# Layer norm of the first stage: row work on 128x128 and squared sums, spread and high part arranged for it, in five rounds

## The reference, cut to what matters

```
def _ln(x, w, b):
    mu = jnp.mean(x, axis=-1, keepdims=True)
    var = jnp.var(x, axis=-1, keepdims=True)
    return (x - mu) * jax.lax.rsqrt(var + EPS) * w + b
...
zn = _ln(z, ln_in_w, ln_in_b)             # z = group norm of x
a = m * jax.nn.sigmoid(zn @ w_ag + b_ag) * (zn @ w_ap + b_ap)
b = m * jax.nn.sigmoid(zn @ w_bg + b_bg) * (zn @ w_bp + b_bp)
p = jnp.einsum('bikc,bjkc->bijc', a, b)
x = _ln(p, ln_out_w, ln_out_b) @ w_z + b_z
g = jax.nn.sigmoid(zn @ w_g + b_g)
return x * g
```

## Time and profile before

| | |
|---|---|
| median of 3 runs | 1107.92 us |
| profiled execution, its own time | 1107.85 us |
| its span (first to last instruction) | 1105.8 us |
| PE busy | 997.5 us (90%) |
| DVE busy | 804.0 us (73%) |
| ACT busy | 681.7 us (62%) |
| POOL busy | 556.9 us (50%) |
| granted TensorE clock, mean | 0.957 |

### The profile page before, as it was taken

One profiled execution on the slowest core, in us unless ns is written; L12 is line 12 of the kernel. 1 busy time (PEld: TensorE's weight loads), 2 busy tenths in 40 slices (PEclk: granted clock), 3 DMA queues, 4 the chain that ended last, 5 costly groups with the idle time before them and its releaser, 6 DMA issues.

```text
span 1105.8 us, 36355 instructions
## 1 busy us (share of the span) xinstructions
PE 997.5 (90%) x14204; PEld 780.1 (71%) x14204; DVE 804.0 (73%) x1270; ACT 681.7 (62%) x1102; POOL 556.9 (50%) x479
## 2 busy tenths in 40 slices
PE   5689798579999999996999997799999999789997
PEld 5543333248898888985999997587878787645554
DVE  6926988976786868767988888664646565567775
ACT  5747565365666656655676765484857667546665
POOL 0000644488092561904777774390937648146664
PEclk9989999869999999998999998799999999989999
DMA  9800000000301203069999760004031130599994
GB/s 349 317 9 1 0 1 0 1 2 4 134 24 78 78 22 134 4 181 231 226 208 203 180 149 1 2 4 154 5 104 54 46 111 4 167 196 285 294 276 153
DMA packets 173196, 121.32 MB, mean 110 GB/s; under 512 B 69764, under 2 KB 152068, under 8 KB 173064
## 3 DMA queue, kind: packets, MB, share of 16 engines
q1 hardware_dynamic: 173064, 119.34, 39.9%
HBM read 68.99 MB, written 50.33 MB: 108 GB/s over the span
## 4 chain that ended last, share of the span: by engine, by line
PE 77%; DVE 9%; DMA 4%; issue 4%; POOL 3%; ACT 2%; SPq 1%; DVEq 0%; POOLq 0%; ACTq 0%
PE PS L486 69%; DMA AB<-x 3%; PE PS L737 3%; PE PS L752 2%; PE PS L784 2%; DVE AB L1259 1%; POOL XT_ALL L994 1%; POOL AB L341 1%; DVE XT_ALL L1280 1%; DMA AB<-k_scratch 1%; PE PS L500 1%; DVE XT_ALL L1443 1%; ACT WK L874 1%; SPq L355 0%; DVE WK L1316 0%
## 5 line engine op out<-in xcount | busy, mean ns | idle before, releaser
L486 PE MATMUL PS<-EFF,XT_ALL 64*128 64x64 f16 (+1 forms) x10368 | 342.6, 201 | 8.7 <-POOL XT_ALL L994 3.6
L486 PEld LDWEIGHTS PS<-EFF,XT_ALL 64*128 64x128 f16 (+1 forms) x10368 | 315.5, 96 | 42.7 <-issue 16.9
L486 PE MATMUL PS<-AB 128*128 128x256 f16 (+3 forms) x1482 | 291.5, 348 | 36.3 <-ACT AB L841 10.6
L486 PEld LDWEIGHTS PS<-AB 128*128 128x128 f16 (+3 forms) x1482 | 200.9, 137 | 124.6 <-issue 34.0
L874 ACT ACTIVATE WK<-PS,T 128x512 f32<-128x512 f32 x256 | 174.7, 685 | 94.9 <-PE PS L486 82.8
L1059 POOL TENSOR_TENSOR AB<-WK,AB 128x512 f32 x128 | 144.8, 1162 | 111.8 <-ACT AB L884 110.8
L341 POOL TENSOR_TENSOR AB<-WK,MS 128x512 f32 x96 | 130.5, 1389 | 104.5 <-DVE WK L1316 104.5
L994 POOL TENSOR_TENSOR XT_ALL<-AB,XT_ALL 128x512 f32 (+1 forms) x59 | 69.8, 1192 | 166.5 <-DVE XT_ALL L1280 156.2
L1069 POOL TENSOR_TENSOR WK<-XT_ALL 128x512 f32 (+1 forms) x64 | 82.0, 1283 | 76.5 <-PE PS L737 51.1
L1324 DVE TENSOR_TENSOR WK<-PS,WK 128x512 f32<-128x512 f32 x128 | 85.8, 686 | 33.2 <-ACT WK L874 33.2
L1316 DVE TENSOR_TENSOR WK<-PS,WK 128x512 f32<-128x512 f32 x128 | 86.8, 688 | 30.1 <-ACT WK L874 23.4
(11 more groups left out here) (193 smaller groups left out, 1537.4 us busy)
## 6 DMA issues: line engine op xcount, KB each, us to landing
AB<-x SPq DMA_DIRECT2D x64, 512.0 KB, 7.0
p_scratch<-WK SPq DMA_DIRECT2D x32, 512.0 KB, 2.6
k_scratch<-WK SPq DMA_DIRECT2D x64, 256.0 KB, 2.1
AB<-k_scratch SPq DMA_DIRECT2D x32, 512.0 KB, 10.4
out<-AB SPq DMA_DIRECT2D x16, 1024.0 KB, 8.6
AB<-p_scratch SPq DMA_DIRECT2D x29, 512.0 KB, 7.6
AB<-p_scratch SPq DMA_DIRECT2D x2, 640.0 KB, 6.3
RAW<-w SPq DMA_DIRECT2D x2, 256.0 KB, 2.7
```

Of the source, the lines that this page charges most:

```text
L486: return nc.tensor.matmul(dst, lhsT, rhs, start=start, stop=stop)
```

## The change

The 64 groups go in five rounds of 13, 13, 13, 13 and 12, all written out (no loops). The squared sums of a group are four float32 products with 32 columns of weights each instead of one with 96: image row r of the group goes to partitions 32r to 32r+31 of bank 0, and only 128 columns wide. So the variances of a round fill a tile of 128x128, and DVE and ACT do the row work on that tile; the three bfloat16 parts now lie side by side on the free axis and are taken from all partitions. The spread of a group is twelve bfloat16 matmuls of 128 columns, with contraction over 64 partitions each: two column halves x, three parts i, and the two partition halves h, which write to two banks. DVE makes the high part by a second multiplication of the centred group with the spread in PSUM, straight to float16, where it copied `zn` before. The centred groups have three PSUM banks instead of four. Two tiles of the first chunk (`project`) now wait for the last round's first row operation.

```
 NB1 = ROWS // PR1
-SPREAD_LAG = 5
-TG = 16
-NT = NG // TG
+SPREAD_LAG = 4
+ROUNDS = (13, 13, 13, 13, 12)
+NT = len(ROUNDS)
+FIRST = [sum(ROUNDS[:t]) for t in range(NT + 1)]
+TG = max(ROUNDS)
+TL = ROUNDS[-1]
+CONST_ROW = 31
+assert FIRST[NT] == NG and 2 * TG <= CONST_ROW
...
-        spread_sb = part(TG * P // 2).bitcast(bf16)
+        spread_sb = part(2 * TG * P // 2).bitcast(bf16)
-        ve, sd, rt, tmp = (part(BANK) for _ in range(4))
-        parts3 = part(BANK // 2).bitcast(bf16)
+        ve, sd, rt, tmp = (part(P) for _ in range(4))
+        parts3 = part(3 * P // 2).bitcast(bf16).rearrange("p (i n) -> p i n", i=3)
...
+        LOWS_V = [u for u in range(TL) if u % 3 == 0]
...
+        def cs_bank(n):
+
+            return PS[:, 1 + n % 3, :]
+
+        def spread_banks(n):
+
+            return PS[:, 4 + n % 2 * 2:6 + n % 2 * 2, 0:2 * P]
...
             def spread_rstd(t, u):
 
+                n = FIRST[t] + u
                 if u == 0:
                     pe.wait_ge(rb_ready, t + 1)
-
-                reached(pe, zn_done, t * TG + max(u - 1, 0))
-                mm(PS[:, 5 + u % 2, :], spread_sb[:, u * P:(u + 1) * P], parts3).then_inc(bc_done, 1)
-
-
-
-            def round_(t):
+                if n >= 2:
+                    pe.wait_ge(zn_done if n - 2 >= NG - TL else hi_done, n - 1)
+                for x in range(2):
+                    for i in range(3):
+                        for h in range(2):
+                            rows = slice(h * CH, (h + 1) * CH)
+                            last = mm(spread_banks(n)[:, h, x * P:(x + 1) * P],
+                                      spread_sb[rows, (x * TG + u) * P:(x * TG + u + 1) * P],
+                                      parts3[rows, i, :], i == 0, i == 2)
+                last.then_inc(bc_done, 1)
+
+            def square_sums(t, v):
+
+                n = FIRST[t] + v
+                pe.wait_ge(sq_ready, n + 1)
+                if v == 0:
+
+                    pe.wait_ge(var_ready, t + 1)
+                s0 = L_SEL + 30 - 2 * v
+                for r in range(GR):
+                    last = nc.tensor.matmul(PS[32 * r:32 * r + 32, 0, 0:P], NCF[:, s0:s0 + 32],
+                                            sq[:, n % 2, r * P:(r + 1) * P], start=v == 0, stop=v == ROUNDS[t] - 1)
+                last.then_inc(mm2_done, 1)
+
+            for t in range(NT):
                 spread = 0
-                for u in range(TG + 1):
-                    if u < TG:
-                        reached(pe, sq_ready, t * TG + (u - 3))
-                        mm(PS[:, u % 4, :], cs, XT[:, ds(t * (TG * GR) + u * GR, GR), :].rearrange("p r n -> p (r n)")
+                for u in range(ROUNDS[t] + 1):
+                    n = FIRST[t] + u
+                    if u < ROUNDS[t]:
+                        reached(pe, sq_ready, n - 2)
+                        mm(cs_bank(n), cs, XT[:, n * GR:(n + 1) * GR, :].rearrange("p r n -> p (r n)")
                            ).then_inc(mm1_done, 1)
                     if u >= 1:
-                        v = u - 1
-                        pe.wait_ge(sq_ready, t * TG + (v + 1))
-                        if v == 0:
-
-                            reached(pe, var_ready, t + 1)
-                        s0 = L_SEL + 30 - 2 * v
-                        mm(PS[0:96, 4, :], NCF[:, s0:s0 + 96], sq[:, v % 2], v == 0, v == TG - 1).then_inc(mm2_done, 1)
-                    if isinstance(t, int) and t == 0:
-                        if u == SPREAD_LAG:
+                        square_sums(t, u - 1)
+                    if t == 0:
+                        if u == 5:
                             fold_weights()
-                        if u == 2 * SPREAD_LAG:
+                        if u == 10:
 
                             small([(PS[:, 7, P:2 * P], ones, diag),
                                    (PS[:, 7, 2 * P:2 * P + 1], out_sq, ones[:, 0:1])])
-                    elif SPREAD_LAG <= u < TG:
-                        for _ in range(1 if (u - SPREAD_LAG) % 2 or u == TG - 1 else 2):
+                    elif u >= SPREAD_LAG:
+                        goal = ROUNDS[t - 1] * (u - SPREAD_LAG + 1) // (ROUNDS[t] - SPREAD_LAG + 1)
+                        while spread < goal:
                             spread_rstd(t - 1, spread)
                             spread += 1
-                assert spread in (0, TG)
-
-            rounds(pe, round_, NT, 2)
+                assert spread in (0, ROUNDS[t - 1])
+
...
                 pe.wait_ge(folded, layer + 1)
                 if layer == 0:
                     pe.wait_ge(lo_done, AHEAD)
+                    pe.wait_ge(var_ready, NT + 1)
                 for n in range(AP):
                     project(0, n, bias=False)
                 if layer == 0:
-                    for u in range(TG):
+                    for u in range(TL):
                         spread_rstd(NT - 1, u)
-                    pe.wait_ge(lo_done, low_count(TG - 1))
+                    pe.wait_ge(lo_done, low_count(TL - 1))
                     pe.wait_ge(lo_done_v, len(LOWS_V))
...
-            def centred(t, last=False):
-                for u in range(TG):
-                    n = t * TG + u
+            for t in range(NT):
+                for u in range(ROUNDS[t]):
+                    n = FIRST[t] + u
...
                     reached(act, mm2_done, n - 1)
-                    nc.scalar.activation(sq[:, u % 2], PS[:, u % 4, :], ACT.Square, bias=T[:, 14:15]
+                    nc.scalar.activation(sq[:, n % 2], cs_bank(n), ACT.Square, bias=T[:, 14:15]
                                          ).then_inc(sq_ready, 1)
...
-                root(t + 2, sd[0:96, :], ve[0:96, :], ahead=last)
-
-            rounds(act, centred, NT, 1, lambda t: centred(t, last=True))
+                root(t + 2, sd, ve, ahead=False)
+
...
-            def normalise(t, last=False):
-
-                dve.wait_ge(mm2_done, t * TG + TG)
-                V.tensor_scalar(ve[0:96, :], PS[0:96, 4, :], EPS, None, ALU.add).then_inc(var_ready, 1)
+            def row_work(t):
+
+                dve.wait_ge(mm2_done, FIRST[t + 1])
+                V.tensor_scalar(ve, PS[:, 0, 0:P], NCF[:, L_EPS:L_EPS + 1], None, ALU.add).then_inc(var_ready, 1)
                 dve.wait_ge(std_ready, t + 2)
-                r, w = rt[0:96, :], tmp[0:96, :]
-                chain(t, V.reciprocal(r, sd[0:96, :]))
-                chain(t, V.scalar_tensor_tensor(w, r, -0.5, r, ALU.mult, ALU.mult))
-                chain(t, V.tensor_tensor(w, w, ve[0:96, :], ALU.mult))
-                chain(t, V.scalar_tensor_tensor(r, w, 1.5, r, ALU.add, ALU.mult))
-
-                reached(dve, bc_done, t * TG)
-                chain(t, V.tensor_copy(parts3[0:96, :], r))
-                chain(t, V.tensor_tensor(r, r, parts3[0:96, :], ALU.subtract))
-                chain(t, V.tensor_copy(parts3[32:64, :], r[32:64, :]))
-                chain(t, V.tensor_copy(parts3[64:96, :], r[64:96, :]))
-                chain(t, V.tensor_tensor(r[64:96, :], r[64:96, :], parts3[64:96, :], ALU.subtract))
-                V.tensor_copy(parts3[64:96, :], r[64:96, :]).then_inc(rb_ready, 1)
-                for u in range(TG):
-                    n = t * TG + u
+                step(V.reciprocal(rt, sd))
+                step(V.scalar_tensor_tensor(tmp, rt, -0.5, rt, ALU.mult, ALU.mult))
+                step(V.tensor_tensor(tmp, tmp, ve, ALU.mult))
+                step(V.scalar_tensor_tensor(rt, tmp, 1.5, rt, ALU.add, ALU.mult))
+
+                reached(dve, bc_done, FIRST[t])
+                step(V.tensor_copy(parts3[:, 0, :], rt))
+                step(V.tensor_tensor(rt, rt, parts3[:, 0, :], ALU.subtract))
+                step(V.tensor_copy(parts3[:, 1, :], rt))
+                step(V.tensor_tensor(rt, rt, parts3[:, 1, :], ALU.subtract))
+                V.tensor_copy(parts3[:, 2, :], rt).then_inc(rb_ready, 1)
+
+            def normalise(t):
+
+                last = t == NT - 1
+                for u in range(ROUNDS[t]):
+                    n = FIRST[t] + u
...
-                    V.tensor_tensor(zn[:, u % 8], XT[:, ds(n * GR, GR), :].rearrange("p r n -> p (r n)"),
-                                    PS[:, 5 + u % 2, :], ALU.mult).then_inc(zn_done, 1)
+                    xt = two(XT[:, n * GR:(n + 1) * GR, :].rearrange("p r n -> p (r n)"))
+                    V.tensor_tensor(two(zn[:, n % 8]), xt, spread_banks(n), ALU.mult).then_inc(zn_done, 1)
                     if not last:
-                        if u > 0:
-                            high(n - 1, (u - 1) % 8)
+                        V.tensor_tensor(two(half(n, 0)), xt, spread_banks(n), ALU.mult).then_inc(hi_done, 1)
                     elif u - 2 in LOWS_V:
                         low(u - 2)
-                if not last:
-                    high(t * TG + TG - 1, (TG - 1) % 8)
-                else:
-                    assert LOWS_V[-1] < TG - 2
+                assert not last or LOWS_V[-1] < ROUNDS[t] - 2
...
```

(15 more changed lines are left out.)

64 lines of the change are left out of this document (21 added, 43 removed).

## The result

The changed kernel takes 1090.4 us (median of 4 executions, 1086.7 to 1090.5) against 1108.1 us for the kernel before: ratio 0.983, 95% interval 0.981 to 0.985. The forecast was 1105.7 with a range from 1091. Its direction was right, though hardly forecast (0.46 faster against 0.42 slower), and its size was not: 17.8 us gained instead of 2.2, just outside the range. The profiled execution is the 1086.7 one, with a span of 1084.9 us; why it is 3.6 us quicker than its fellows is a question of its own, taken up with the experiments.

The account below looks back on a forecast made before the run. DVE was taken to bound the kernel, PE close behind; PE's new load eats DVE's gain within rounds (31.6 us for 13 groups), and the shorter end moves 236.86 to 234.7: 2.2 us gained, 1105.7 us, range 1091 to 1122.

Parts of the forecast that it names:

- What bounds the kernel: Before 236.9 us: DVE sets the pace, 33.05 of a 38.0 us round, with PE close behind at 33.88.
- DVE's part: Row work 3.9 us instead of 10.1, a group 1.3 instead of 1.65; DVE is out of the lead.
- PE's part: PE's new prices per group: `mm1` 1.06 us, squared sums 0.75, spread 0.46.
- The change of shape: PE switching between `mm1` and the sums or spread, which use other array shapes: 0.10 us more.
- late second load: Second weight load of `mm1` behind sums or spread comes 0.10 us late; 0.025 in each column strip of the sums.
- The squared sums: PE, every group: column strips run two at a time, 0.65 us plus 0.10 for shape, 0.75; bounds 0.22 to 1.69.
- The turn: Between rounds: a chain from last sums over spread, DVE products, EPS, root and ACT to next sums, 6.1 us.
- The strips cost less: Rival, PE: changes between column strips and full array are free, sums 0.55, `mm1` 0.86; 1090 us, chance 0.18.
- One after another: Rival, PE's sums: column strips do not run side by side; 1122 us, or 1126 by the skill's rule; chance 0.25.
- The clock at each turn: Rival, between rounds: PE's clock falls after idling, about 1.7 us lost at each of four turns; 1112.5, chance 0.13.
- main case: Whole kernel: the prediction's own sum, 1105.7 us, own range 1100 to 1109, chance 0.44.
- The first round and the end: First row work from 92.8 us, held by DVE's weight preparation; last from 217.4, PE's last low part at 234.7.

Follow-up runs that it names:

- e1: Changed kernel with each of a group's four squared-sum products using 128 columns of weights (whole array, no column strips): 1118.7 us, ratio 1.008 to the kernel before.
- e2b: Changed kernel with all four squared-sum products in strip 0, except in each round's last group (normalised values wrong): 1122.0 us, ratio 1.012 to the kernel before.
- e5: Changed kernel with the spread's twelve products using weights on all 128 rows instead of two row tiles of 64: 1104.3 us, ratio 0.996 to the kernel before.
- after_again: Changed kernel measured once more, unchanged: 1091.4 us (1090.5 to 1092.6).
- after_third: Changed kernel measured again, unchanged, on the same chip as a run with unused products filling idle TensorE: 1092.3 us (1089.7 to 1093.8).
- e4: Changed kernel with the high part again a copy of the first product, one group later, instead of a second product: 1099.5 us, ratio 0.993 to the kernel before.

## Why the prediction was off, step by step

**What bounds the kernel** held: DVE out of the lead and waiting for PE, which sets the pace of every round (e1, e2b and e5 load PE alone, and make the kernel 14 to 32 us longer). That DVE waits in every group did not: it doesn't behind two spreads in a row.

**DVE's part** held: row work 4.1 (3.9 forecast; the reciprocal 0.95 against 0.84, the root 0.31 against 0.35), a group 1.20 (1.3).

**PE's part** failed in one term. The change of shape (0.10) and the late second load (0.10) are as read from the earlier trace rows: `mm1` takes 1.05 between sums and spread, 0.86 in e1 where nothing changes shape. The spread at 0.44 held. The squared sums failed. The prediction took 0.65 for them, from "the second pass of strip r goes with the first of strip r+1", plus a late load in each strip, and 0.10 for the change. Measured are 0.36 in all, so 0.26 for themselves. The arithmetic assumed an order of passes (first and second of one strip, then the next) and two at a time, because the earlier trace rows show two row strips. The trace has four passes at once, which must be those of four strips, and then the other four: two slots of 0.13 instead of five of 0.11, and hardly any load to be seen (eight loads in 0.16, alongside). The lower bound was 0.22 and was "all four strips at once"; the value taken was three times that, and it was the row tiles' evidence for two at a time that pulled it there.

**What that term is worth.** Between first and last sums of a round stand twelve at 0.39 less, 4.7 us, of which 0.65 goes back where PE now waits for ACT in the last group. The turn, with the thirteenth in it, is 5.3 instead of 6.1. So 31.6 becomes 26.8; measured are 26.7. The last row work comes at 197.8 instead of 217.4, 19.6 us earlier, and 47 sums at 0.39 are 18.3. The prediction had the sensitivity right (47 sums times a small price), and its own line for it, "if less than 0.55, it is clearly faster", was met by what stood there.

**The rivals.** "The strips cost less" gave 1090 and is closest to the measured 1090.4, but its reason was wrong: the changes of shape are not free, 0.20 a group. It agrees by luck, because two errors offset each other. It has 0.55 and 0.86 for sums and `mm1`, the trace 0.36 and 1.05, both 1.41 together. "One after another" is what e2b builds: 1122.0, the very number forecast for it, but by luck too, since the sums take 0.99 there and not 1.09, which is 5 us less, and the clock falls behind its first two turns, whose rounds take 36.6 us where the third takes 33.8. The rule of the Trainium skill ("TensorE: Matmul & The Clock Gate", Part 3, What overlaps and what doesn't) that a load overlaps running matmuls only where the row group differs gave the prediction's estimate of 1126. The traces here do not follow it: eight loads are done in 0.16 us beside passes over the same 128 rows (121.40 to 121.56), and in e2b eight passes in one strip take 0.89 us in all (0.99 with the change of shape), so that no load adds to them.

**The clock at each turn** was given 0.13 and a price of 1.7 a turn. It happens, after 2.1 to 3.3 us of idle time, at three turns in each of two profiles of the changed kernel and at none in the first. By the rounds it costs 1.4 to 2.4 a turn, and filling the idle time gets back 6.2 us. How many of the unprofiled executions it hits is not shown. As a cause it was independent of the main case, and it should not have been a rival to it but a term of the sum with its own chance.

**The first round and the end.** The first row work came at 91.6 for 92.8, bound by DVE's weight preparation as said. But the cheaper sums shorten the groups ahead of that preparation too: without half clock in the first round it comes at 89.7 and 89.4 (after_again, after_third). From the last row work to the next stage 17.7 against 17.3 forecast (18.5 in the other two profiles): held. That the stage behind keeps its length held as well.

## What to carry to other kernels

Products with few weight columns, spread over different column strips of the array, run together: four cost little more than one, and the same four in one strip cost four. Where a term stands in every group, its lower bound deserves a case of its own with its own chance, and a range that reaches it. Between phases, look at what the first operation of the next phase waits for on each engine: moving one small operation ahead of four large ones was worth 6 to 7 us here, and filling 2 us of idle TensorE 6. The two do not add up, since the first also takes away most of the idle time that the second fills.

## What the runs showed of the hardware that was not expected

- Four column strips with the same 128 rows run at once: eight float32 passes of 128 columns in 0.26 us, against 0.89 in one strip or over the whole array. The first four passes start together, the other four 0.13 us later; that these are first and second passes of each strip is inferred.
- A copy of 128x512 float32 from SBUF to float16 on DVE takes 0.42 us while POOL is idle, and 1.0 to 1.1 while POOL works, as in the earlier trace rows; a product with an operand in PSUM takes 0.68 either way. So more than half of the old copy's price goes with POOL's work. That holds for all copies of e4: 0.42 for the eleven with POOL idle, up to 1.01 beside it. Rows of e4, in order of time:

```profile
128.71 0.42 DVE L1301 CAST XT_ALL<-AB 128x512 f16<-128x512 f32 x1
...
129.21 1.16 POOL L1023 TENSOR_TENSOR XT_ALL<-AB,XT_ALL 128x512 f16<-128x512 f32 x1 [10.71 <-DVE XT_ALL L1301]
...
140.95 1.00 DVE L1301 CAST XT_ALL<-AB 128x512 f16<-128x512 f32 x1
```

- Idle time of 2.1 to 3.3 us on TensorE is followed by half clock in some executions and not in others of the same kernel, so that a single profile can show either.
